# One product fewer for Bu: B's high and low parts as the two halves of one weight matrix

## The reference

```
x = x + layernorm(mixer(layernorm(x)))
x = x + layernorm(experts(layernorm(x)))

mixer(u):   Bu = u @ B_w.T                       # 64 states per token
            h  = Re( causal convolution of Bu[:, n] over time with eig[n] ** t )   # |eig[n]| = 1
            y  = h @ C_w.T + D * u
experts(x): router = softmax(x @ w_router); gate = softmax(x @ w_gating / 0.1)
            g, up, down of 8 experts of 512 hidden units: sum_e w[e] * (silu(x @ Wg[e]) * (x @ Wu[e])) @ Wd[e]
            w = router * gate / sum(router * gate)
```

## Time and profile before

| | |
|---|---|
| median of three runs | 1120.02 us |
| the profiled execution, its own time | 1119.97 us |
| its span in the trace | 1118.2 us |
| TensorE matmul busy | 1100.1 us, 98% |
| VectorE busy | 918.4 us, 82% |
| ScalarE busy | 743.5 us, 66% |
| GpSimd busy | 702.4 us, 63% |
| first `g` matmul of chunk 0, of chunk 1 | at 31.64 us, at 105.73 us |
| chunks 1 to 13, start to start | 66.9 us each |

### The profile page before, as it was taken

The page is one execution under the profiler, slowest core; times in us unless marked ns, Lnnn a source line. Parts: engine busy times, 40 slices in busy tenths (PEclk is TensorE's granted clock), DMA queues, the critical chain, the costliest instruction groups (busy, mean ns, idle before and its releaser), DMA issues.

```text
span 1118.2 us, 16871 instructions
## 1 busy us (share of the span) xinstructions
PE 1100.1 (98%) x4807; PEld 896.9 (80%) x4807; DVE 918.4 (82%) x1779; ACT 743.5 (66%) x1430; POOL 702.4 (63%) x885
## 2 busy tenths in 40 slices
PE   8999999999999999999999999999999999999997
PEld 4677888888888888888888888888888888888885
DVE  7799888797888979888897888979888897887855
ACT  6676676757667576676757667576676757666563
POOL 1586765748567485765748567585766748556453
PEclk9999999999999999999999999999999999999999
DMA  4340413213142222313213132232313313231110
GB/s 137 96 120 13 114 48 82 79 40 104 39 102 69 67 70 63 96 47 92 72 40 100 44 100 66 69 75 52 101 48 96 75 40 94 47 87 48 48 48 20
DMA packets 182333, 79.66 MB, mean 71 GB/s; under 512 B 124608, under 2 KB 160096, under 8 KB 182240
## 3 DMA queue, kind: packets, MB, share of 16 engines
q1 hardware_dynamic: 182240, 78.57, 26.2%
HBM read 59.14 MB, written 19.40 MB: 70 GB/s over the span
## 4 chain that ended last, share of the span: by engine, by line
PE 92%; DVE 4%; ACT 1%; issue 1%; POOL 0%; DMA 0%; POOLq 0%; ACTq 0%; SPq 0%; DVEq 0%
PE u L372 10%; PE u L374 10%; PE g L372 10%; PE u L373 10%; PE g L374 10%; PE g L373 10%; PE y L372 10%; PE y L374 10%; PE y L373 10%; DVE hid L1029 1%; ACT gate L691 0%; DVE hid_lo L1035 0%; PE n_ps L465 0%; PE n_ps L466 0%; PE m_ps L372 0%
## 5 line engine op out<-in xcount | busy, mean ns | idle before, releaser
L1349 POOL TENSOR_TENSOR hid_lo<-hid,hid_hi 128x512 fp32r<-128x512 f32 x255 | 333.5, 1308 | 339.4 <-ACT hid_hi L697 339.4
L691 ACT ACTIVATE gate<-g 128x512 f32<-128x512 f32 x512 | 305.9, 598 | 315.2 <-PE g L374 314.4
L1029 DVE TENSOR_TENSOR hid<-gate,u 128x512 f32<-128x512 f32 x512 | 348.3, 681 | 179.3 <-ACT gate L691 142.4
L697 ACT ACTIVATE hid_hi<-hid 128x512 fp32r<-128x512 f32 x512 | 320.0, 625 | 32.4 <-DVE hid L1029 30.7
L1035 DVE TENSOR_TENSOR hid_lo<-hid,hid_hi 128x512 fp32r<-128x512 f32 x257 | 217.8, 848 | 0.2
L372 PE MATMUL u<-xe_hi,w_hi 128*128 128x512 f32 x512 | 200.0, 391 | 1.6 <-DVE hid L1029 1.5
L372 PE MATMUL g<-xe_hi,w_hi 128*128 128x512 f32 x512 | 199.6, 390 | 0.1
L374 PE MATMUL u<-xe_hi,w_lo 128*128 128x512 f32 x512 | 199.3, 389 | 0.0
L372 PE MATMUL y<-hid_hi,w_hi 128*128 128x512 f32 x512 | 199.3, 389 | 0.0
L374 PE MATMUL g<-xe_hi,w_lo 128*128 128x512 f32 x512 | 199.3, 389 | 0.0
L373 PE MATMUL g<-xe_lo,w_hi 128*128 128x512 f32 x512 | 199.3, 389 | 0.0
(11 more groups left out here) (234 smaller groups left out, 1168.7 us busy)
## 6 DMA issues: line engine op xcount, KB each, us to landing
cw_b<-cw_scratch SPq DMA_DIRECT2D x128, 256.0 KB, 3.3
x_sb<-x_in SPq DMA_DIRECT2D x16, 256.0 KB, 3.1
out_scratch<-acc_t SPq DMA_DIRECT2D x60, 64.0 KB, 1.9
ffn<-out_scratch SPq DMA_DIRECT2D x15, 256.0 KB, 2.7
x_out<-o_sb SPq DMA_DIRECT2D x15, 256.0 KB, 2.2
xn_scratch<-mix_t SPq DMA_DIRECT2D x56, 64.0 KB, 2.2
feat<-xn_scratch SPq DMA_DIRECT2D x14, 256.0 KB, 2.6
y_scratch<-mix_t SPq DMA_DIRECT2D x56, 64.0 KB, 1.9
```

The lines of the kernel that those rows point to most:

```text
L691: nc.scalar.activation(gate[:, k % 2, :], g_ps[k % 2][:], ACT.Silu).then_inc(gate_ready, 1)
L697: nc.scalar.activation(hid_hi[:, slot(c, k), :], hid[:, slot(c, k), :], ACT.Copy).then_inc(hi_ready, 1)
L1029: nc.vector.tensor_tensor(hid[:, slot(c, k), :], gate[:, k % 2, :], u_ps[k % 2][:], ALU.mult).then_inc(hid_ready, 1)
L1349: nc.gpsimd.tensor_tensor(hid_lo[:, slot(c, k), :], hid[:, slot(c, k), :], hid_hi[:, slot(c, k), :].bitcast(f32), ALU.subtract).then_inc(l ...
```

## The change

Bu is made by two matmuls. The weight that was `[B_hi | B_hi]` is now `[B_hi | B_lo]` and is multiplied with the high part of the data; the second weight, which was `[B_lo | B_lo]`, is now `[0 | B_hi]` and is multiplied with the low part. The upper 64 rows of `m_ps` then hold the large term and the lower 64 rows the two small terms. ScalarE moves the lower rows to SBUF (`mix_move_b`), VectorE adds them to the upper rows in PSUM (`mix_merge`), and `enter` becomes two multiplications of 64 rows, both from the upper rows: by the cosines into the upper half of `v_sb`, by the sines into the lower half. In the usual body `move_b` and `merge` are issued in the unit of `bu` (19), `enter_cos` in 20 and `enter_sin` in 21; scan, leave, move_sines, fold, hi_w, lo_w, c, y and block_y go one unit later each. In `FIRST_X_AT` the new steps stand in units 7 and 8 and nothing else moves. In `SECOND_X_AT` the steps from scan to y go one unit later and `block_y` of chunk 2 goes into unit 0 of chunk 1.

```diff
-X_AT = {... "bu": 19, "enter": 20, "scan": 21, "leave": 22, "move_sines": 23, ...
+X_AT = {... "bu": 19, "move_b": 19, "merge": 19, "enter_cos": 20, "enter_sin": 21, "scan": 22, "leave": 23, ...
...
-                exact(m_ps[:], proj_hi[:, 0:P], proj_lo[:, 0:P], act_hi[:], act_lo[:]).then_inc(bu_ready, 1)
+                nc.tensor.matmul(m_ps[:], proj_hi[:, 0:P], act_hi[:], start=True, stop=False)
+                nc.tensor.matmul(m_ps[:], proj_lo[:, 0:P], act_lo[:], start=False, stop=True).then_inc(bu_ready, 1)
...
+            def mix_move_b(c):
+                act.wait_ge(bu_ready, c + 1)
+                nc.scalar.activation(b_small, m_ps[NS:P, :], ACT.Copy).then_inc(b_moved, 1)
...
-            nc.scalar.activation(proj_hi[:], proj[:, 0:P + D], ACT.Copy)
+            nc.scalar.activation(proj_hi[:, 0:NS], proj[:, 0:NS], ACT.Copy)
+            nc.scalar.activation(proj_hi[:, P:], proj[:, P:P + D], ACT.Copy)
+            nc.scalar.activation(proj_lo[:, NS:P], proj[:, 0:NS], ACT.Copy)
...
-            def mix_enter(c):
-                dve.wait_ge(bu_ready, c + 1)
+            def mix_merge(c):
+                dve.wait_ge(b_moved, c)
+                nc.vector.tensor_tensor(m_ps[0:NS, :], m_ps[0:NS, :], b_small, ALU.add).then_inc(bu_merged, 1)
+
+            def mix_enter_cos(c):
+                dve.wait_ge(bu_merged, c)
                 if c == 1:
                     dve.wait_ge(cw_t_ready, 1)
-                nc.vector.tensor_tensor(v_sb[:], m_ps[:], trig[:], ALU.mult).then_inc(mix_link, 1)
+                nc.vector.tensor_tensor(v_sb[0:NS, :], m_ps[0:NS, :], trig[0:NS, :], ALU.mult)
+
+            def mix_enter_sin(c):
+                nc.vector.tensor_tensor(v_sb[NS:P, :], m_ps[0:NS, :], trig[NS:P, :], ALU.mult).then_inc(mix_link, 1)
...
+                        nc.vector.memset(proj_lo[:, 0:NS].bitcast(f32), 0.0)
...
-            nc.gpsimd.tensor_tensor(proj_lo[:], proj[:, 0:P + D], proj_hi[:].bitcast(f32),
+            nc.gpsimd.tensor_tensor(proj_hi[:, NS:P], proj[:, 0:NS], proj_hi[:, 0:NS].bitcast(f32), ALU.subtract)
+            nc.gpsimd.tensor_tensor(proj_lo[:, P:], proj[:, P:P + D], proj_hi[:, P:].bitcast(f32),
                                     ALU.subtract).then_inc(proj_split, 1)
```

More of the change, by code:

```diff
@@ L44 @@
 X_AT = {"load_x": 0, "stats_x": 4, "norm_x": 6, "scale_x_a": 9, "scale_x_b": 10, "block_x": 11, "hi_x": 16, "du": 17,
-        "lo_x": 17, "bu": 19, "enter": 20, "scan": 21, "leave": 22, "move_sines": 23, "fold": 23, "hi_w": 24, "lo_w": 25,
-        "c": 27, "y": 28, "block_y": 30}
+        "lo_x": 17, "bu": 19, "move_b": 19, "merge": 19, "enter_cos": 20, "enter_sin": 21, "scan": 22, "leave": 23,
+        "move_sines": 24, "fold": 24, "hi_w": 25, "lo_w": 26, "c": 28, "y": 29, "block_y": 31}
 Y_AT = {"stats_y": 6, "norm_y": 8, "z_a": 11, "z_b": 12, "residual": 12, "stats_x1": 14, "norm_x1": 15, "scale_x1_a": 18,
         "scale_x1_b": 19, "block_xe": 20, "hi_xe": 25, "lo_xe": 26, "logits": 28, "softmax": 29, "peak": 30, "silus": 31}
-FIRST_X_AT = {"scale_x_a": 0, "scale_x_b": 1, "turn_x": 3, "hi_x": 4, "du": 4, "lo_x": 5, "bu": 7, "enter": 8, "scan": 9,
+FIRST_X_AT = {"scale_x_a": 0, "scale_x_b": 1, "turn_x": 3, "hi_x": 4, "du": 4, "lo_x": 5, "bu": 7, "move_b": 7, "merge": 7, "enter_cos": 8, "enter_sin": 8, "scan": 9,
               "leave": 10, "move_sines": 11, "fold": 11, "hi_w": 12, "lo_w": 12, "c": 14, "y": 15}
@@ L54 @@
 SECOND_X_AT = {"stats_x": 5, "norm_x": 6, "scale_x_a": 11, "scale_x_b": 12, "block_x": 13, "hi_x": 18, "du": 19, "lo_x": 19,
-               "bu": 21, "enter": 22, "scan": 23, "leave": 24, "move_sines": 25, "fold": 25, "hi_w": 26, "lo_w": 27,
-               "c": 29, "y": 30, "block_y": 31}
+               "bu": 21, "move_b": 21, "merge": 21, "enter_cos": 22, "enter_sin": 23, "scan": 24, "leave": 25, "move_sines": 26,
+               "fold": 26, "hi_w": 27, "lo_w": 28, "c": 30, "y": 31}
+LATE_Y_AT = {"block_y": 0}
 OWN_AT = {"exps": 0, "products": 1, "weights": 2}
@@ L66, in stages @@
         return [(1, FIRST_X_AT), (1, FIRST_Y_AT), (2, SECOND_X_AT)]
+    if b == 1:
+        return [(2, LATE_Y_AT), (2, Y_AT), (3, X_AT)]
     return [(c, at) for c, at in ((b + 1, Y_AT), (b + 2, X_AT)) if c < NCHUNK]
@@ L167, in build @@
         w_sin = sum_sb[0:NS, :]
+        b_small = sum_sb[0:NS, :]
         cw_t = acc_t[0:SMALL, :]
@@ L187, in build @@
         parts_ready, sines_moved = sem("parts_ready"), sem("sines_moved")
+        b_moved, bu_merged = sem("b_moved"), sem("bu_merged")
         first_link = sem("first_link")
@@ L759, in body @@
                             mix_du(m)
+                        if k == at.get("move_b"):
+                            mix_move_b(m)
                         if k == at.get("move_sines"):
@@ L1129, in _ @@
             dve.wait_ge(trig_ready, 1)
-            mix_enter(0)
+            early_enter()
             mix_scan(0)
@@ L1227, in body @@
                             mix_lo_x(m)
-                        if k == at.get("enter"):
-                            mix_enter(m)
+                        if k == at.get("merge"):
+                            mix_merge(m)
+                        if k == at.get("enter_cos"):
+                            mix_enter_cos(m)
+                        if k == at.get("enter_sin"):
+                            mix_enter_sin(m)
                         if k == at.get("scan"):
```

3 lines of the change are left out of this document (added).

## The result

The changed kernel is slower: 1123.02 us median over 9 runs (1121.75 to 1126.41), against 1120.1 us for nine runs of the kernel before on the same chip (1119.94 to 1122.1). The ratio is 1.0025, with a 95% interval of 1.0016 to 1.0034. The forecast was 1117.8 us with a range up to 1120.3, so it was wrong by more than 5 us, and in sign. The runs of the changed kernel also lie further apart than those of the kernel before, 4.7 us against 2.2; the part on the failed step comes back to that. Every ratio in this text, here and under the experiments, is to runs of the kernel before on the same chip. Two executions far outside all others, one of `two_only` of 2165.85 us and one of the kernel before of 6380.79, are left out of every median given.

What follows compares the result with a forecast made beforehand. TensorE's matmul count was taken to bound chunks from 1 on, partly VectorE's queue chunk 0. Terms -2.95 - 0.23 + 1.0 = -2.18 us from 1119.97 gave 1117.79, median 1117.8 us; range 1116.5 to 1120.3.

Steps and rivals of the forecast that it cites:

- The matmul that goes: One bu matmul fewer in each of bodies 1 to 13, 0.227 us each: 2.95 us of TensorE's time.
- What is added per bu: ScalarE gets a 0.59 us copy; VectorE a merge and second half of enter, about 1.2 us more work.
- Units 19 to 26 of the later chunks: Shifted mixer steps in later chunks: scan waits behind GpSimd, but TensorE does not wait at unit 26's u.
- the branch that was given as the first: Later chunks: the leave goes before GpSimd, unit 24's hid ends at 359.1, leaving 1.5 us before unit 26's u.
- The step that failed, first: Later chunks, units 24 to 31: a permutation, same queue for units 1 to 3, no TensorE waits; -2.95 us.
- The step that failed, second: Chunk 0's second pass: merge free in unit 22, other shifts cancel within 0.3 us, matmul kept: -0.23 us.
- The first pass: Chunk 0's first pass: VectorE's queue runs later, unit 13's u is delayed: +1.0 us, saved matmul used up.
- Before the loop: Before the loop: ScalarE's three small pieces, some 0.3 us more, and other additions stand before waits: 0.
- Rival two: One more lost turn in each pass of chunk 0, about 2.2 us above forecast, 1120.0 us; chance 0.21.
- Rival three: Unit 23's leave loses its turn in all 13 bodies, unit 26's u waits: 6.5 us, 1124.3 us; chance 0.07.
- Rival four: Later chunks: TensorE waits about as much as the matmul saved; chunk 0's +1.0 remains: 1121.0 us; chance 0.09.
- Rival one: Everything hidden, chunk 0's turns fall better, all 15 matmuls count: 3.40 us, 1116.6 us; chance 0.20.

Runs made afterwards that it cites:

- two_only: The kernel before with one of bu's three products left out, nothing added or moved: 1117.23 us, ratio 0.9972.
- twice: The changed kernel with bu's first product made twice, so three matmuls per bu again: 1126.02 us, ratio 1.0052.
- y28: The changed kernel with only y of the usual bodies put back from unit 29 to unit 28: 1119.12 us, ratio 0.999.
- merge22: The changed kernel with the merge of chunk 0's second pass in unit 22 instead of 21: 1123.35 us, ratio 1.0028.
- copy22: The changed kernel with y in unit 28 and, in chunk 0's second pass, copy and merge in unit 22 instead of 21: 1118.53 us, ratio 0.9983.
- two_only_again: The kernel before with one of bu's three products left out, nothing added, run once more for a profile: 1117.01 us.
- both: The changed kernel with y in unit 28; in chunk 0, second-pass copy and merge in unit 22, first-pass merge in unit 8: 1117.99 us, ratio 0.9979.

## Why the prediction was wrong

**The matmul that goes: right.** 13 x 0.227 = 2.95 us; shown by `two_only`, by `twice` and by the eight chunks of 66.69 us.

**What is added per bu: right.** One copy of 0.60 us, a merge of 0.69, a second half of enter. The sines' half starts 0.69 us after the cosines' (53.68 after 52.99) and holds the next back by 0.72 (54.40), where the step between full-height rows here is 0.60. So two halves take 1.41 us, 0.8 more than enter's 0.59 and not 0.6: the rule of the Trainium skill (VectorE: DVE Perf Modes, Two Vector instructions with no wait between them) agrees with the trace on both sides of the half.

**Units 19 to 26 of the later chunks: right, in the branch that was given as the first.** VectorE and TensorE in chunk 4, which starts at 308.02:

```profile
355.92 1.90 DVE L909 TENSOR_TENSOR_SCAN sum_sb<-v_sb 128x512 f32<-128x512 f32 x1
...
359.38 0.69 DVE L913 TENSOR_TENSOR m_ps<-sum_sb,trig 128x512 f32<-128x512 f32 x1
359.98 0.67 DVE L1054 TENSOR_TENSOR hid<-gate,u 128x512 f32<-128x512 f32 x1
...
362.20 0.39 PE L377 MATMUL u<-xe_hi,w_hi 128*128 128x512 f32 x1
```

The scan is long behind GpSimd (1.90 us, forecast some 2.1), the leave is first and short, `hid` of unit 24 ends at 360.65 and `u` of unit 26 starts at 362.20. The room is 1.55 us, forecast 1.5.

**The step that failed, first.** "In units 24 to 28 the rest is a permutation of what was there" and "block_y in unit 31 ends just before unit 0's hid is due, so the tight units 1 to 3 see the same queue as before", and with them "Later chunks: -2.95 us", in which waits of TensorE are put at nothing. (The sentence "Either way TensorE does not wait" was on unit 26, and it held.) I looked at the new steps and at their place, and took what follows as a permutation. But y had moved from unit 28 into 29, behind an addition that meets GpSimd to within 0.01 us. The kernel before had that encounter too, in a row that I had not looked at, because it never cost anything there: 0.23 us, 14 times out of 14. It cost nothing because it was always won, and `y28` shows that a loss would have cost nothing either as long as y stood ahead. The change took away both covers at once: c in unit 28 made the turn one that is lost at times, and y in unit 29 made the loss cost time. The measured part is the five long chunks, 3.1 us in the profiled execution. Without them it would have been 1121.75 - 3.1 = 1118.65 us. By 0.62 us each, and if nothing else differed, the median of 1123.0 would stand for about seven long chunks of 13 and the 1126.4 for twelve or thirteen. These counts are estimates: no slower execution of this kernel has a trace, and kernels in which no lost turn is paid for spread by up to 1.6 us (`y28`) or 2.2 (the kernel before) themselves.

**The step that failed, second.** "The merge falls into unit 22, before the residual addition, which takes 1.20 us because it waits for GpSimd; 0.5 to 0.6 us of that were waiting, so the merge is free", and "These cancel within 0.3 us: 0, and the matmul is kept, -0.23". Measured: +0.93 us. I had put only VectorE's merge into the account of unit 22, and not ScalarE's copy, which stands ahead of the unit's gate and makes `hid` and the residual late; in `merge22` `hid` waits for the gate with no merge ahead of it, and with the copy moved too (`copy22`) the residual addition is short again. The addition then missed its turn by 0.04 us. And the leave, a unit later than it was, now comes 0.23 us behind GpSimd's `hid_lo` (1.78 us against 0.69 before, where it came 0.02 us ahead of GpSimd's addition); no edit here mended that. The matmul was not kept there either (`two_only_again`: +0.03 us in chunk 0 with two matmuls less).

**The first pass: nearly right.** +0.74 against +1.0, with each start within 0.1 us.

**Before the loop: right in sum.** No row showed the 0.3 us for ScalarE's three pieces. They took from 6.14 to 6.73 us, where the one piece took from 6.45 to 6.85, and the first `g` matmul starts at 31.60 us against 31.64.

**The rivals.** Rival two (one more lost turn in each pass of chunk 0, 0.21) is what the second pass did: +1.16 against the forecast, at about the 1.1 us that it had for one pass. In the first pass it did not occur. Rival three, the slower one at 0.07, had the kind and sign of what happened, `hid` late in later chunks, but in the wrong place: it looked at units 24 and 26 and charged all 13 bodies or none, as if each chunk ran the same; one with a tie of 0.01 us in it does not. Its reason against, that one lost turn alone does not do it, held for unit 24, but in unit 29 one lost turn with y behind it does it. Rival four (0.09) had nearly the amount, 3.1 us of waiting against the 2.95 gained, but not the mechanism: it had each chunk lose what it gained, whereas eight chunks kept all of it and five were held up by nearly three times as much. Rival one did not occur.

## What to carry to other kernels

When steps move by a unit, look not only where they stand but at every operation that they now stand behind, and ask of each operation with two SBUF inputs how close GpSimd's comes to it: two that start within 0.01 us of each other in the trace can come out the other way once a step elsewhere has moved, however regularly one of them won before (14 of 14 here). Price such a tie as lost in some chunks, with the room at the tightest unit downstream, and keep nothing queued between it and the next operation that TensorE waits for. A copy on a third engine counts as much as the added work on the engine looked at, if that engine also makes what the others wait for.

## What the runs showed of the hardware

- A turn is lost whole, whatever the size of the loser: a 128x64 addition went from 0.23 to 1.36 us for coming 0.01 us late, about as long as GpSimd's 128x512 one beside it (1.28 us). When VectorE won, GpSimd paid only 0.1 us (1.39), since the addition it stood behind is short; behind a 128x512 one it paid 0.5 (1.74 and 1.80). The Trainium skill (SBUF — State Buffer, SBUF: two separate sides) gives the lock and its whole-instruction hold, and the rows agree. It also gives the lock to the one that starts first; below 0.01 us the traces don't bear that out, for GpSimd starts 1 to 6 ns ahead in all 14 encounters of the changed kernel's profile, and VectorE has the turn in nine of them.
- The scan, whose two inputs are both `v_sb`, takes part in these turns (2.31, 1.90 and 1.22 us for the same 128x512 form), while the merge and the sines' half of enter, which read PSUM beside SBUF, had a mean of 0.69 us over all 15 bodies.
- With the same program, executions of the changed kernel differed by 4.7 us, and those of kernels in which no lost turn is paid for, as far as their traces show, by 0.5 (`both`), 1.6 (`y28`) and 2.2 us (the kernel before). That lost turns make the difference is likely, but not shown, since only one of the nine executions has a trace.
